# A recommendation tower on one core: ScalarE's and VectorE's orders redone around the pair copies, the first and the last pick, and the last relus

## The chip, the cores and the metric

The kernel runs on one core of a Trainium2 chip. The number that counts is the device time of one execution in microseconds (us). TensorE (PE), VectorE (DVE), ScalarE (ACT), GpSimd (POOL) and SyncE (SP) each work through their own list of instructions in order; they meet only at semaphores. PE's weight loads are shown as an engine of their own, PEld.

## The reference, cut to what matters

For each of 512 samples, 26 rows of 128 numbers are looked up by id (one per table) and joined by the dense vector to 27 vectors; the 351 products of two different ones are the features of a three-layer network.

```python
e = stack([tbl_f[ids[:, f]] for f in range(26)], axis=1)            # 512 x 26 x 128
all_vecs = concatenate([r_dense_proj[:, None, :], e], axis=1)        # 512 x 27 x 128
interactions = einsum('bnd,bmd->bnm', all_vecs, all_vecs)            # upper triangle: 351
h = concatenate([r_dense_proj, interact_flat, r_dense_proj], axis=1) # 512 x 607
h = maximum(h @ W_top1 + b_top1, 0)                                  # 512 x 512
h = maximum(h @ W_top2 + b_top2, 0)                                  # 512 x 256
y = h @ W_top3                                                       # 512 x 1
```

## The kernel before, in words

**Two ways to look up.** Fifteen tables are gathered by 60 indirect DMAs of POOL (4 tiles of 128 samples, 15 tables; line 227). They arrive with samples on partitions and are turned by PE (`turn`, line 270), then copied into `vecs` by ACT or, for two groups of the last tile, by DVE (`place_turned`, lines 454 and 587). The other eleven tables of 1000 rows are *picked*: a table lies in SBUF as 125 partitions x 8 rows, DVE compares the id's offset with 0 to 7 (`compare`, line 633) and PE multiplies the table with those one-hot columns (`pick`, line 255). A table goes through as a high part, which ACT casts (`split_table`, line 468), and a low part, which DVE subtracts (`make_low`, line 623); so a pick is 8 + 8 matmuls of 512 columns. The offsets come from `spread` (PE, line 242: ids laid over 125 partitions) and `find_offset` (ACT, line 460, which also needs `minus_first`, a small DMA). Until its first real work PE multiplies zeros (`keep_warm`, line 236).

**The last pick** (`LAST`, table 10 of the eleven) is done in two halves of 256 columns, with products of tile 0 between them, since tiles 0 and 1 need only the first half. Its one-hot columns are made 512 wide, as for every other pick.

**Then four tiles of 128 samples**, t = 0 to 3: `products` (line 293, 512 small matmuls of 27 x 27 in all) fills the bank pair `gram[t % 2]`; ACT (blocks of samples j = 0, 2) and DVE (j = 1, 3) copy the wanted rows into `pairs` in three layers of copies (`pairs_first` 8, `pairs_second` 8, `pairs_third` 4 copies per engine; line 445); `layer1` (lines 314 and 319) makes four slices of 128 hidden units in turn in two banks `shared[0]`, `shared[1]`, each emptied by an ACT relu (`relu1`, line 512); `layer2` (lines 334 and 342) and DVE's `relu2` (line 575); `layer3` (line 359) and `place_y` (line 581). In tiles 0 and 3 ACT takes one of DVE's copies over (`act_helps`).

**What sets the order.** The order of every engine is written out by hand, at the end of its block. A wait in the list holds up everything behind it on that engine. Layer 1's slice s needs the relu of slice s - 2 (same bank) and, in tiles 1 and 2, `relu2` of the tile before; its first slice waits for both engines' pair copies.

## Time and profile before

| | |
|---|---|
| runs of the kernel | 112.75, 113.46, 117.8 us (median 113.46) |
| profiled execution, its own time | 112.97 us |
| its span in the trace | 111.2 us |
| granted TensorE clock, mean | 0.998 of full speed |
| PE busy | 98.9 us (89%) |
| DVE busy | 75.0 us (67%) |
| ACT busy | 66.0 us (59%) |
| POOL busy | 62.4 us (56%) |

The busy shares are averages over unlike stages: up to about 53 us the picks, from there to 94 us the tiles, then a last stretch with nothing left to overlap. A row of the timeline gives start and duration in us, engine, line and operation, and in brackets the idle time before it and what ended it.

### The profile page before, as it was taken

What the parts mean: (1) busy time and instruction counts of PE and PEld (TensorE: products, weight loads), DVE (VectorE), ACT (ScalarE), POOL (GpSimd) and SP (SyncE); (2) the same over time, 40 slices, a digit from 0 to 9 for tenths busy, and PEclk for the clock granted to TensorE, in tenths of its full rate; (3) what the DMA queues carried; (4) which work ended last, traced back from release to release, by engine and by line L of the source; (5) the groups of instructions that cost most, each with busy time, mean ns of one, the idle gap of its engine ahead of it and who ended that gap; (6) DMA issues with size and microseconds to landing.
All of it is one profiled execution on the core that took longest, in us unless ns stands there. A gap on an engine that the chain in (4) does not pass through costs nothing.

```text
span 111.2 us, 3639 instructions
## 1 busy us (share of the span) xinstructions
PE 98.9 (89%) x1532; PEld 79.5 (72%) x1532; DVE 75.0 (67%) x205; ACT 66.0 (59%) x149; POOL 62.4 (56%) x68
## 2 busy tenths in 40 slices
PE   5999999999999999999789559889979997954982
PEld 2346667888887888888678459878978997924970
DVE  5269999899999999999006931992797200993021
ACT  3178999396468468446306994993797311595310
POOL 3877777777877777777777677767750000000000
PEclk9999999999999999999999999999999999999999
DMA  2899885476667679962222123222220000000000
GB/s 46 207 290 229 237 221 150 146 178 134 206 156 142 214 203 327 370 230 53 55 68 56 49 53 72 52 53 56 56 68 0 0 6 6 0 0 6 0 0 1
DMA packets 4936, 12.22 MB, mean 110 GB/s; under 512 B 2061, under 2 KB 2061, under 8 KB 4792
## 3 DMA queue, kind: packets, MB, share of 16 engines
q1 hardware_dynamic: 2848, 8.03, 24.7%
q0 software_dynamic: 1920, 3.94, 14.8%
q8 instruction: 12, 0.20, 0.8%
q10 hardware_dynamic: 152, 0.02, 0.2%
q14 instruction: 4, 0.03, 0.1%
HBM read 11.98 MB, written 0.00 MB: 108 GB/s over the span
## 4 chain that ended last, share of the span: by engine, by line
PE 69%; ACT 21%; DMA 4%; issue 3%; DVE 1%; ACTq 1%
PE shared L255 38%; ACT pairs L445 15%; PE gram L293 9%; PE shared L319 8%; DMA minus_first<-in_minus_first 4%; PE shared L334 4%; PE turned L270 3%; PE shared L314 2%; ACT h L512 2%; ACT vecs L454 2%; PE gram L342 1%; PE gram L242 1%; ACT vecs L477 1%; PE turned L359 1%; ACT table_hi L468 1%
## 5 line engine op out<-in xcount | busy, mean ns | idle before, releaser
L227 POOL DMA_INDIRECT rows<-in_tbl,ids x60 | 61.4, 1024 | 19.0 <-issue 18.0
L633 DVE TENSOR_SCALAR onehot<-offset 125x512 fp32r<-125x512 f16 x88 | 33.1, 435 | 3.7 <-ACT offset L460 2.9
L445 DVE COPY pairs<-gram 27x128 f32<-27x128 f32 (+6 forms) x78 | 22.6, 290 | 18.3 <-PE gram L293 17.1
L255 PE MATMUL shared<-onehot,table_hi 125*128 125x512 f32 (+1 forms) x96 | 26.2, 391 | 0.1
L445 ACT COPY pairs<-gram 27x128 f32<-27x128 f32 (+6 forms) x82 | 20.9, 255 | 9.1 <-PE gram L293 8.1
L255 PE MATMUL shared<-onehot,table_lo 125*128 125x512 f32 (+1 forms) x96 | 24.6, 378 | 0.0
L255 PEld LDWEIGHTS shared<-onehot,table_hi 125*128 125x128 f32 x96 | 16.8, 188 | 4.8 <-ACT table_hi L468 0.6
L255 PEld LDWEIGHTS shared<-onehot,table_lo 125*128 125x128 f32 x96 | 17.0, 188 | 4.2 <-DVE table_lo L623 0.7
L319 PE MATMUL shared<-pairs,w 128*128 128x128 f32 x128 | 17.0, 276 | 2.7 <-ACT pairs L445 2.7
L468 ACT CAST table_hi<-table 125x1024 fp32r<-125x1024 f32 x11 | 11.6, 1056 | 11.2 <-PE shared L255 10.4
L319 PEld LDWEIGHTS shared<-pairs,w 128*128 128x128 f32 x128 | 15.6, 192 | 2.9 <-ACT pairs L445 2.9
L293 PE MATMUL gram<-vecs 128*27 128x27 f32 x1024 | 12.3, 193 | 3.8 <-issue 2.3
L293 PEld LDWEIGHTS gram<-vecs 128*27 128x27 f32 x1024 | 10.5, 104 | 6.1 <-issue 4.3
L623 DVE TENSOR_TENSOR table_lo<-table,table_hi 125x512 fp32r<-125x512 f32 x22 | 14.8, 677 | 0.0
L472 ACT COPY vecs<-shared 128x512 f32<-128x512 f32 x10 | 12.2, 1218 | 1.5 <-PE shared L255 1.5
L512 ACT ACTIVATE h<-shared,b 128x128 f32<-128x128 f32 x16 | 5.7, 368 | 11.4 <-PE shared L319 11.4
L454 ACT COPY vecs<-turned 128x512 f32<-128x512 f32 (+1 forms) x14 | 9.4, 681 | 1.6 <-PE turned L270 1.5
L270 PE MATMUL turned<-identity,rows 128*128 128x128 f32 x60 | 9.4, 276 | 0.0
L314 PE MATMUL shared<-dense,w_dense 128*128 128x128 f32 x32 | 6.6, 287 | 1.8 <-ACT vecs L477 1.2
L270 PEld LDWEIGHTS turned<-identity,rows 128*128 128x128 f32 x60 | 7.1, 141 | 1.3 <-issue 0.4
L460 ACT ACTIVATE offset<-gram,minus_first 125x512 f16<-125x512 f32 x9 | 5.8, 685 | 2.6 <-DMA minus_first<-in_minus_first 2.6
L314 PEld LDWEIGHTS shared<-dense,w_dense 128*128 128x128 f32 x32 | 4.9, 191 | 2.2 <-issue 1.2
(36 smaller groups left out, 43.6 us busy)
## 6 DMA issues: line engine op xcount, KB each, us to landing
table<-in_tbl SPq DMA_DIRECT2D x11, 448.0 KB
w<-in_w_pairs SPq DMA_DIRECT2D x1, 1024.0 KB
rows<-in_tbl,ids POOLq DMA_INDIRECT x60, 3.6
table<-in_tbl SPq DMA_DIRECT2D x11, 52.0 KB
w_dense_both<-in_w_dense SPq DMA_DIRECT2D x1, 512.0 KB, 5.3
w<-in_w SPq DMA_DIRECT2D x1, 512.0 KB, 7.5
dense<-in_dense_t SPq DMA_DIRECT2D x1, 256.0 KB, 6.5
ids<-in_ids SPq DMA_DIRECT2D x1, 30.0 KB, 1.9
```

The source lines that it names most:

```text
L227: pool.indirect_dma_start(rows[:, t, f, :], None, a[f"tbl_{GATHER_TABLES[f]}"], bass.IndirectOffsetOnAxis(ids[:, t, f:f + 1], 0)).then_inc ...
L255: last = nc.tensor.matmul(out, (table_hi, table_lo)[part][u % 2][:, c, :], onehot[half][:, c - half * PIECE, cols], start=half == 0 and pa ...
L270: last = nc.tensor.transpose(turned[k % 2][:, u * 128:(u + 1) * 128], rows[:, t, f0 + u, :], identity[:, :])
L293: last = nc.tensor.matmul(gram[t % 2][32 * j:32 * j + VECS, o0:o0 + VECS], x, x, start=True, stop=True)
L314: nc.tensor.matmul(out, w1_dense[:, o], dense[:, cols], start=True, stop=False)
L319: last = nc.tensor.matmul(out, w1[:, c, o], pairs[:, c, cols], start=False, stop=c == CHUNKS - 1)
L445: last = copy(to[:, :, :, j, :], src[:, first:first + CHUNKS, :, :])
L454: nc.scalar.copy(vecs[:, t * TILE:(t + 1) * TILE, 1 + f0:1 + f0 + n], turned[k % 2][:, 0:n * 128].rearrange("d (n b) -> d b n", n=n)).then ...
L468: nc.scalar.copy(table_hi[u % 2][:, :, :], table[u % TABLE_BUFS][:, :, :]).then_inc(table_hi_ready, 1)
L472: nc.scalar.copy(vecs[:, :, 1 + GATHERED + u], shared[u % 2][:, :]).then_inc(picked_placed, 1)
L623: nc.vector.tensor_tensor(table_lo[u % 2][:, part, :], table[u % TABLE_BUFS][:, part, :], table_hi[u % 2][:, part, :].bitcast(fp32), ALU.s ...
L633: nc.vector.tensor_scalar(onehot[half][:, k, :], offset[:, u, :], float(half * PIECE + k), None, ALU.is_equal).then_inc(onehot_ready, 1)
```

## The change

ScalarE's list is rearranged: the pair copies of tiles 1 to 3 are cut into groups of four to eight, and relus of layer 1 and turned rows stand between the groups. `act_helps` goes: both engines make 20 pair copies in every tile. PE places `turn(3, 2)` ahead of `layer2(1)`, and `turn(3, 1)` between two halves of `layer1(1)`; slice 0 of `layer1(0)` no longer waits for the second half of the last pick. At the start, six warm-up matmuls, `spread(0)`, then five more, then the other spreads. The last pick's compares are 256 columns wide, the first 256 of all eight first. At the end the last tile's second relu goes to ACT, and layer 3's second part is cut in two (`Y_TILES`), one copied by ACT, one by DVE.

**ScalarE, tiles 1 and 2** (`h1_0`, `h1_1`: outputs of layer 1's relu for even and odd tiles; `gram1` holds the products of tile 1, `gram0` those of tile 2). Before, from tile 2's first copies on:

```order
L445 COPY pairs<-gram0 27x4x2x16 x8
L454 COPY vecs<-turned0 128x128x4
L512 ACTIVATE h1_1<-shared0,b1 128x128
L512 ACTIVATE h1_1<-shared1,b1 128x128
L445 COPY pairs<-gram0 19x4x2x16 x2
L445 COPY pairs<-gram0 22x4x2x16 x2
L445 COPY pairs<-gram0 10x4x2x16 x2
L445 COPY pairs<-gram0 14x4x2x16 x2
L512 ACTIVATE h1_1<-shared0,b1 128x128
L512 ACTIVATE h1_1<-shared1,b1 128x128
```

Now:

```order
L454 COPY pairs<-gram0 27x4x2x16 x4
L463 COPY vecs<-turned0 128x128x4
L516 ACTIVATE h1_1<-shared0,b1 128x128
L454 COPY pairs<-gram0 27x4x2x16 x4
L516 ACTIVATE h1_1<-shared1,b1 128x128
L454 COPY pairs<-gram0 19x4x2x16 x2
L454 COPY pairs<-gram0 22x4x2x16 x2
L516 ACTIVATE h1_1<-shared0,b1 128x128
L454 COPY pairs<-gram0 10x4x2x16 x2
L454 COPY pairs<-gram0 14x4x2x16 x2
L516 ACTIVATE h1_1<-shared1,b1 128x128
L463 COPY vecs<-turned0 128x128x4
```

The first relu of tile 1 stands behind four copies instead of eight, and each later one behind four more; the turned rows (3, 2) have come ahead of the tile's last four copies.

**TensorE, tile 1's second layer** (`turned0`, `turned1`: the two banks of turned rows, here groups (3, 1), (3, 2) and (3, 3)). Before, from slice 3 of `layer1(1)`:

```order
L314 MATMUL shared1<-dense,w1_dense 128x128
L319 MATMUL shared1<-pairs,w1 128x128 x4
L270 MATMUL turned1<-identity,rows 128x128 x4
L334 MATMUL shared0<-h1_1,w2 128x128 x4
L334 MATMUL shared1<-h1_1,w2 128x128 x4
L270 MATMUL turned0<-identity,rows 128x128 x4
L314 MATMUL shared0<-dense,w1_dense 128x128
```

Now:

```order
L318 MATMUL shared1<-dense,w1_dense 128x128
L323 MATMUL shared1<-pairs,w1 128x128 x4
L273 MATMUL turned0<-identity,rows 128x128 x4
L338 MATMUL shared0<-h1_1,w2 128x128 x4
L338 MATMUL shared1<-h1_1,w2 128x128 x4
L318 MATMUL shared0<-dense,w1_dense 128x128
```

Turn (3, 2), which stood behind the second layer of tile 1, now stands ahead of it; turn (3, 1) has gone up between slices 1 and 2.

**VectorE, the last pick** (`onehot0`, `onehot1`: one-hot columns for rows 0 to 3 and 4 to 7 of a partition). Of the change:

```order
L632 TENSOR_TENSOR table_lo0<-table1,table_hi0 125x512
L641 TENSOR_SCALAR onehot0<-offset 125x256 x4
L632 TENSOR_TENSOR table_lo0<-table1,table_hi0 125x512
L641 TENSOR_SCALAR onehot1<-offset 125x256 x4
L641 TENSOR_SCALAR onehot0<-offset 125x256 x4
```

Four more of `onehot1` follow. Before there were two groups of four, each 125x512, in the places of the first two.

The diff, cut to what the prediction speaks of:

```diff
-Y_TILES = [(0, 2), (2, 4)]
+Y_TILES = [(0, 2), (2, 3), (3, 4)]
-WARM_UPS = 9
+WARM_UPS = (6, 5)
-        y_sum = turned[0][0:1, :]
+        y_sum = [turned[0][0:1, :], turned[0][0:1, :], turned[1][0:1, :]]
@@ layer1
-                    pe.wait_ge(picked_placed, PICKED + 1)
                 for s in slices:
-                    if s < 2 and 1 <= t <= 2:
+                    if s < 2 and t == 0:
+                        pe.wait_ge(picked_placed, PICKED + s)
+                    elif s < 2 and t <= 2:
                         pe.wait_ge(h2_ready, S2 * (t - 1) + s + 1)
@@ TensorE's order
-            keep_warm(WARM_UPS, shared[0])
+            keep_warm(WARM_UPS[0], shared[0])
             pe.wait_ge(chooser_ready, 1)
             pe.wait_ge(pick_ids_half_ready, 1)
-            for u in range(SPREAD_BANKS):
+            spread(0)
+            keep_warm(WARM_UPS[1], shared[0])
+            for u in range(1, SPREAD_BANKS):
                 spread(u)
-            keep_warm(3, shared[1])
+            keep_warm(2, shared[1])
...
-            layer1(1)
+            layer1(1, [0, 1])
             turn(3, 1)
+            layer1(1, [2, 3])
+            turn(3, 2)
             layer2(1)
-            turn(3, 2)
...
             layer3(1)
+            layer3(2)
@@ ScalarE's order
             relu1(0, [0, 1])
-            pairs_first(1)
             place_turned(2, 2)
-            relu1(0, [2])
+            pairs_first(1, [0, 1])
             place_turned(2, 3)
-            relu1(0, [3])
+            relu1(0, [2, 3])
+            pairs_first(1, [2, 3])
             pairs_second(1)
             pairs_third(1)
-            pairs_first(2)
+            pairs_first(2, [0, 1])
             place_turned(3, 0)
-            relu1(1, [0, 1])
-            pairs_second(2)
-            relu1(1, [2, 3])
+            relu1(1, [0])
+            pairs_first(2, [2, 3])
+            relu1(1, [1])
+            pairs_second(2, [2, 3])
+            relu1(1, [2])
+            pairs_second(2, [0, 1])
+            relu1(1, [3])
+            place_turned(3, 2)
             pairs_third(2)
-            place_turned(3, 2)
-            relu1(2, [0, 1])
-            relu1(2, [2])
+            relu1(2, [0, 1, 2])
+            pairs_first(3)
             relu1(2, [3])
-            pairs_first(3)
             pairs_second(3)
             pairs_third(3)
             relu1(3)
+            act.wait_ge(h2_sum_ready, S2 * TILES)
+            nc.scalar.activation(h2[:, 1, 3 * TILE:4 * TILE], h2_sum(3, 1), ACT.Relu,
+                                 bias=b2[:, 1:2]).then_inc(h2_act_ready, 1)
+            act.wait_ge(y_sum_ready, 2)
+            nc.scalar.copy(y[:, Y_TILES[1][0] * TILE:Y_TILES[1][1] * TILE],
+                           y_sum[1][:, Y_TILES[1][0] * TILE:Y_TILES[1][1] * TILE]).then_inc(y_ready, 1)
@@ VectorE's order, the last pick
+            dve.wait_ge(offset_ready, PICKED)
+            make_low(LAST, 0)
+            compare(LAST, 0, slice(0, BATCH // 2))
+            make_low(LAST, 1)
+            compare(LAST, 1, slice(0, BATCH // 2))
+            compare(LAST, 0, slice(BATCH // 2, BATCH))
+            compare(LAST, 1, slice(BATCH // 2, BATCH))
...
-            relu2(3)
-            place_y(1)
+            relu2(3, [0])
+            place_y(2)
```

## Rows read from the trace of the kernel before

**Rows 1.** The chain that ended last, shares of the span by engine and line.

```profile
PE shared L255 38%; ACT pairs L445 15%; PE gram L293 9%; PE shared L319 8%; DMA minus_first<-in_minus_first 4%; PE shared L334 4%; PE turned L270 3%; PE shared L314 2%; ACT h L512 2%; ACT vecs L454 2%; PE gram L342 1%; PE gram L242 1%; ACT vecs L477 1%; PE turned L359 1%; ACT table_hi L468 1%
```

**Rows 2.** Timeline, the start: start, duration (us), engine, instruction, idle before.

```profile
1.20 3.94 PE L236 MATMUL shared<-blank 128*128 128x512 bf16 x9 [1.20 <-DVE blank L636]
...
3.23 0.35 DVE L640 CAST pick_ids_half<-pick_ids 11x512 f16<-11x512 int32 x1
...
5.80 0.69 ACT L460 ACTIVATE offset<-gram,minus_first 125x512 f16<-125x512 f32 x1 [2.62 <-DMA minus_first<-in_minus_first]
```

**Rows 3.** Timeline, the last pick.

```profile
48.62 1.47 DVE L633 TENSOR_SCALAR onehot<-offset 125x512 fp32r<-125x512 f16 x4
...
50.61 1.54 DVE L633 TENSOR_SCALAR onehot<-offset 125x512 fp32r<-125x512 f16 x4
...
51.21 1.39 PE L255 MATMUL shared<-onehot,table_hi 125*128 125x256 f32 x4
...
52.91 0.49 PE L270 MATMUL turned<-identity,rows 128*128 128x128 f32 x3
53.10 0.67 ACT L477 COPY vecs<-shared 128x256 f32<-128x256 f32 x1 [1.40 <-PE shared L255]
```

**Rows 4.** Groups by form: VectorE's copies of turned rows.

```profile
L587 DVE COPY vecs<-turned 128x512 f32<-128x512 f32 x1 | 0.7, 691 | 0.0
...
L587 DVE COPY vecs<-turned 128x384 f32<-128x384 f32 x1 | 0.6, 559 | 1.5 <-PE turned L270 1.5
```

**Rows 5.** Timeline, tile 0's pair copies and first layer.

```profile
59.17 3.04 DVE L445 COPY pairs<-gram 27x128 f32<-27x128 f32 x10 [6.42 <-PE gram L293]
...
64.80 0.66 ACT L477 COPY vecs<-shared 128x256 f32<-128x256 f32 x1
...
65.91 1.06 PE L319 MATMUL shared<-pairs,w 128*128 128x128 f32 x8
```

**Rows 6.** Timeline, up to tile 2's products.

```profile
70.84 1.06 PE L319 MATMUL shared<-pairs,w 128*128 128x128 f32 x8
...
72.59 1.82 PE L293 MATMUL gram<-vecs 128*27 128x27 f32 x128 [0.69 <-ACT vecs L454]
```

**Rows 7.** Timeline, tile 2's pair copies and tile 1's layers.

```profile
78.50 6.09 DVE L445 COPY pairs<-gram 27x128 f32<-27x128 f32 x20 [1.57 <-PE gram L293]
...
80.64 0.65 ACT L454 COPY vecs<-turned 128x512 f32<-128x512 f32 x1
...
81.17 0.63 ACT L512 ACTIVATE h<-shared,b 128x128 f32<-128x128 f32 x2
...
81.59 0.49 PE L314 MATMUL shared<-dense,w_dense 128*128 128x128 f32 x2 [0.63 <-ACT h L512]
...
84.65 2.05 PE L334 MATMUL shared<-h,w 128*128 128x128 f32 x16
...
86.98 0.39 PE L314 MATMUL shared<-dense,w_dense 128*128 128x128 f32 x2
```

**Rows 8.** Timeline and POOL's line over 60 to 90 us: the gathers.

```profile
77.60 0.94 POOL L227 DMA_INDIRECT rows<-in_tbl,ids  x1 [0.30 <-issue]
...
DMA to landing us min/median/max: 2.4/2.5/3.7
```

**Rows 9.** Timeline, tile 3's pair copies.

```profile
94.22 5.81 DVE L445 COPY pairs<-gram 27x128 f32<-27x128 f32 x19 [5.04 <-PE gram L293]
...
95.85 5.60 ACT L445 COPY pairs<-gram 27x128 f32<-27x128 f32 x21
...
101.50 1.16 PE L319 MATMUL shared<-pairs,w 128*128 128x128 f32 x8 [2.73 <-ACT pairs L445]
```

**Rows 10.** Timeline, the end.

```profile
107.61 0.61 DVE L575 TENSOR_SCALAR h<-gram,b 128x128 f32<-128x128 f32 x2 [6.62 <-PE gram L342]
108.11 1.02 PE L359 MATMUL turned<-h,w 128*1 128x256 f32 x4 [0.31 <-DVE h L575]
109.17 0.41 DVE L581 COPY y<-turned 1x256 f32<-1x256 f32 x1 [0.95 <-PE turned L359]
```

More of the change, by code:

```diff
@@ L155, in build_dlrm @@
         gram_ready = sem("gram_ready")
-        quarter_free = sem("quarter_free")
+        h2_act_ready = sem("h2_act_ready")
         layer_act = sem("layer_act")
@@ L243, in spread, with pick @@
                                  ).then_inc(spread_ready, 1)
-            def pick(u, half, cols=slice(0, BATCH), bank_no=None):
+            def pick(u, half, cols=slice(0, BATCH), bank_no=None, earlier=None):
+                made = PER_PART * (u if earlier is None else earlier)
                 out = shared[u % 2 if bank_no is None else bank_no][:, cols]
@@ L251, in pick @@
                         if part == 0:
-                            pe.wait_ge(onehot_ready, PER_PART * u + c + 1)
+                            pe.wait_ge(onehot_ready, made + c + 1)
                         elif c % LOW_PART == 0:
@@ L352, in layer3 @@
                     pe.wait_ge(turned_act, turns_before(NG * TILES, False))
+                elif k == 1:
+                    pe.wait_ge(y_ready, 1)
                 else:
-                    pe.wait_ge(y_ready, k)
+                    pe.wait_ge(turned_dve, turns_before(NG * TILES, True))
                 cols = slice(t0 * TILE, t1 * TILE)
                 for o in range(S2):
-                    pe.wait_ge(h2_ready, S2 * (t1 - 1) + o + 1)
-                    last = nc.tensor.matmul(y_sum[:, cols], w3[:, o:o + 1], h2[:, o, cols],
+                    if k == 2 and o == 1:
+                        pe.wait_ge(h2_act_ready, 1)
+                    else:
+                        pe.wait_ge(h2_ready, S2 * (t1 - 1) + o + 1)
+                    last = nc.tensor.matmul(y_sum[k][:, cols], w3[:, o:o + 1], h2[:, o, cols],
                                             start=o == 0, stop=o == S2 - 1)
@@ L397, in _ @@
             pe.wait_ge(picked_placed, PICKED - 1)
-            pick(LAST, 0, second, (LAST + 1) % 2)
+            pick(LAST, 0, second, (LAST + 1) % 2, PICKED)
             products(0, 1)
-            pick(LAST, 1, second, (LAST + 1) % 2).then_inc(picked_ready, 1)
+            pick(LAST, 1, second, (LAST + 1) % 2, PICKED).then_inc(picked_ready, 1)
             turn(2, 0)
@@ L431, in _ @@
             layer3(1)
-        def act_helps(t):
-            return t in (0, TILES - 1)
+            layer3(2)
         def put_pairs(copy, t, js, layer, q):
@@ L498, in pairs_third @@
                 put_pairs(nc.scalar.copy, t, (0, 2), 2, 2)
-                last = put_pairs(nc.scalar.copy, t, (0, 2), 2, 3)
-                if act_helps(t):
-                    act.wait_ge(quarter_free, t // (TILES - 1) + 1)
-                    last = put_pairs(nc.scalar.copy, t, (1,), 2, 2)
-                last.then_inc(pairs_act, 1)
+                put_pairs(nc.scalar.copy, t, (0, 2), 2, 3).then_inc(pairs_act, 1)
             def relu1(t, slices=range(S1)):
-                if t >= 2:
+                if t >= 2 and slices[0] == 0:
                     act.wait_ge(h2_sum_ready, S2 * (t - 1))
@@ L568, in _, with relu2 @@
             relu1(3)
+            act.wait_ge(h2_sum_ready, S2 * TILES)
[4 more added lines that the diff above has]
+                           y_sum[1][:, Y_TILES[1][0] * TILE:Y_TILES[1][1] * TILE]).then_inc(y_ready, 1)
         @block.vector
         def _(dve):
-            def relu2(t):
-                for o in range(S2):
+            def relu2(t, sums=range(S2)):
+                for o in sums:
                     dve.wait_ge(h2_sum_ready, S2 * t + o + 1)
@@ L580, in place_y @@
                 cols = slice(Y_TILES[k][0] * TILE, Y_TILES[k][1] * TILE)
-                nc.vector.tensor_copy(y[:, cols], y_sum[:, cols]).then_inc(y_ready, 1)
+                nc.vector.tensor_copy(y[:, cols], y_sum[k][:, cols]).then_inc(y_ready, 1)
             def place_turned(t, g):
@@ L607, in pairs_third @@
                 dve.wait_ge(layer_dve, 2 * t + 2)
-                if act_helps(t):
-                    put_pairs(nc.vector.tensor_copy, t, (1,), 2, 3).then_inc(quarter_free, 1)
-                    put_pairs(nc.vector.tensor_copy, t, (3,), 2, 2)
-                    put_pairs(nc.vector.tensor_copy, t, (3,), 2, 3).then_inc(pairs_dve, 1)
-                else:
-                    put_pairs(nc.vector.tensor_copy, t, (1, 3), 2, 2)
-                    put_pairs(nc.vector.tensor_copy, t, (1, 3), 2, 3).then_inc(pairs_dve, 1)
+                put_pairs(nc.vector.tensor_copy, t, (1, 3), 2, 2)
+                put_pairs(nc.vector.tensor_copy, t, (1, 3), 2, 3).then_inc(pairs_dve, 1)
             def make_low(u, i):
@@ L625, in make_low, with compare @@
                                         ).then_inc(table_lo_ready, 1)
-            def compare(u, half):
+            def compare(u, half, cols=slice(0, BATCH)):
                 if u >= 1:
@@ L632, in compare @@
                 for k in range(PIECE):
-                    nc.vector.tensor_scalar(onehot[half][:, k, :], offset[:, u, :], float(half * PIECE + k),
+                    nc.vector.tensor_scalar(onehot[half][:, k, cols], offset[:, u, cols], float(half * PIECE + k),
                                             None, ALU.is_equal).then_inc(onehot_ready, 1)
@@ L645, in _ @@
             make_low(0, 1)
-            for u in range(1, PICKED):
+            for u in range(1, PICKED - 1):
                 make_low(u, 0)
```

## The prediction, made before the changed kernel ran

> **What bounds the kernel now.** I read the chain of waits first, then the timeline around each edit. The chain [rows 1] is PE's picks for 38% of the span; behind them PE's layers take turns with ACT's pair copies (15%) on one path. So the picks give nothing unless a wait sits in them, and in the tiles the question is each time which of three lists, PE's, ACT's or DVE's, is late. The timeline gives, by place: the first offset ends a wait for `minus_first` [rows 2]; the last pick's third group of matmuls is stretched [rows 3]; `layer1(0)`, `products(2, 0)` and `layer1(1)` wait for work on ACT [rows 5 to 7]; in tile 3 ACT ends the copies 7.28 us after DVE began them [rows 9].
>
> **Base.** The profiled execution took 112.97 us, 1.8 more than its span; the median of the runs shown is 113.46. The sum goes against 112.97. About 2% (2.3 us) is what a measurement of this kernel can tell from no change.
>
> **The start: 0.** Nine warm-ups come 0.43 us apart from 1.20 on, so `spread(0)` starts at 5.07. Behind six it starts at 3.8, the ids being ready at 3.58. But the offset at 5.80 ended its wait with `minus_first`'s landing [rows 2], which nothing here moves. Ids alone would be worth at most the three warm-ups, 1.3; so 0 to 1.3, and I take 0, by the row's own releaser. The other spreads come later; PE has slack until the first table is cast.
>
> **The last pick: 0.9.** Its last four compares start at 50.61 and come (1.54 - 0.44) / 3 = 0.36 apart, so the third group of four matmuls, 51.21 [rows 3], takes 1.39 instead of about 0.64 (4 x 0.117 and the last one's tail): PE stands 0.75 to 0.9 behind its data. No row shows a compare of 256 columns. Bounds: the full pitch of 0.35, then nothing is gained (0), and the size's share. DVE's copies of 512 and 384 columns differ by 132 ns [rows 4], so 0.16 of 0.69 is fixed; a compare's 0.44 then has 0.27 that goes with the columns, and half of it off leaves a pitch of 0.21 to 0.22. The first four end at 49.6, `make_low` at 50.1, the next four by 51.1, as PE gets there. PE runs through, the turn at 52.91 comes at 52.0: 0.9. Second halves, eight more compares, are done by 52.8 and the dense weights by 53.5; PE wants the former at 54.7. The Trainium skill ("VectorE: DVE Perf Modes", the TRN2 errata) speaks against this edit: every operation out of SBUF pays a fixed latency again, so small ones should be avoided; it gives 150 cycles as the fixed term measured. By that a half compare takes about 0.29 us (an estimate from that page), and with nothing of it overlapped this term would be 0.8, not 0.9.
>
> **Tile 0: 0.6.** Pair copies start 0.9 earlier, 58.3. DVE's 20 copies take 6.09 (as in [rows 7]) and set the end, 64.38; ACT's 20 at 0.267 ((5.60 - 0.26) / 20, [rows 9]) end at 63.6. Before, `layer1(0)` waited for all of the last pick, placed by ACT at 64.80 to 65.46 behind 21 copies, and began its pair matmuls at 65.91 [rows 5]. Now slice 0 needs the pairs alone and its dense matmul runs ahead: 64.41. 1.5 earlier in all, 0.6 of it new. Slice 1 needs ACT's placing, done by 64.3.
>
> **Up to `products(2, 0)`: 0.8.** Before, PE's slice 3 was issued by 71.73 (70.84 and 8 x 0.111), then PE waited to 72.59 for turned rows (2, 3) [rows 6], behind eight copies, a turned copy and a relu. Shifted by 1.5 PE is there at 70.23. ACT now: turn (2, 2) out at 67.85, placed by 68.4 (0.53, the step from 80.64 to 81.17 in [rows 7]), four copies to 69.5, rows (2, 3) by 70.1. No wait: 70.25, 2.3 earlier. The deferred relus end at 70.8; `layer2(0)` wants them at 72.2. ACT's other 16 copies end at 75.1, before tile 2's products.
>
> **Tile 1's layers: 0.6.** Tile 2's copies start at 78.50 - 2.34 = 76.16. PE: slices 0 and 1 no longer wait for eight copies; slice 1 out at 78.5, turn 78.9, slices 2 and 3 by 81.2, turn (3, 2) by 81.6. ACT from 76.16: four copies (1.07), turned rows (0.53), relu (0.26), then three times four copies and a relu (1.33 each; the last relu in full, 0.37): 82.1. So `layer2(1)` starts at 82.15, not 84.65, and the turn of 0.44 that stood behind it is gone: `layer1(2)` begins at 84.04, not 86.98 [rows 7]. 2.94 earlier, 0.6 of it new. Here ACT is late by 0.5; behind that relu wait only the turned rows and four copies, done at 83.6, wanted at 84.3. DVE ends its copies at 82.25 and its turned rows at 82.9, in time for `relu2(1)`.
>
> **Tile 3's copies: 1.15.** To `products(3, 1)` nothing else changes: DVE starts at 91.28. Both engines start together now; DVE's 20 take 6.09 and end at 97.37, ACT's, with slice 3's relu among them, at 96.9. The pair matmuls start at 97.41 instead of 101.50 [rows 9]: 4.1.
>
> **The end: 0.5.** Before, second sum to span end: relu twice, four passes of 256 columns (0.22 each and a tail), a copy of 256: 1.97 from 107.61 [rows 10]. Now layer 3's tile 2 fills PE while both relus run side by side; its own 128 columns cost 0.45 and a tail of 0.17, the copy about 0.28. Some 1.47: 0.5, with 0.2 to 0.6 as ends.
>
> **Sum:** 0 + 0.9 + 0.6 + 0.8 + 0.6 + 1.15 + 0.5 = 4.6 (rounded). 112.97 - 4.6 = **108.4 us**, span 106.6. ACT, DVE and PE each lose slack; what is late next is DVE, whose 20 copies at 0.305 end every tile's copies.
>
> **Rivals.**
> 1. *ACT's mixed list becomes the bound* (chance 0.13). Each relu in it waits for PE and holds copies behind it. For it: the relu that releases `layer2(1)` is 0.5 late even in my sum. Against: ACT's 20 copies are 0.75 shorter than DVE's. If relus, once mixed, miss their slots, the terms of 0.8 and 0.6 are lost, and with some of the last pick's: 110.0 to 110.7.
> 2. *The start pays too* (0.12): in executions where `minus_first` lands sooner, the ids are what is late, and up to 1.3 comes off. For: both are within 0.8 us of one another. Against: the releaser named. Gathers cap it: turn (3, 2)'s rows are issued up to 77.60 and land 2.5 later, 80.1 [rows 8], and it runs at 81.2 in my sum: 107.3.
> 3. *Gathers stop PE ahead of `layer2(1)`*, the side of slower (0.03; another 0.06 for a loss that ends within 2%). POOL's rate is fixed by its own 60 instructions, and turn (3, 2), which had 6 us of slack, now has 1.1 and stands in front of the second layer; ACT's placing of it stands in front of the last four copies of tile 2. Past 1.1 each us of lateness costs one: with the slowest landing shown, 3.7 [rows 8], 0.1. To be slower than before the rows must land 4.6 + 1.1 us late, 8.2 us after issue; at 113.5 and more that is slower, from 115.3 it would be measurable. The profile has no such landing. 
>
> The main case has the rest, 0.62; alone it holds 107.6 to 109.3.
>
> **Numbers.** The time is the main case's, 108.4. Range 107.2 to 110.3: below by the gathers' cap, above by the loss of the last pick or of one tile's term and half of another's; it leaves out the worse half of rival 1 and rival 3. Faster by over 2% (under 110.7 against the profiled execution) is the main case, rivals 2 and 4, and most of 1: 0.88. Within 2%: 0.09. Slower: 0.03.
>
> **What would show it.** The first offset still released by `minus_first`, near 5.8. The third group of the last pick under 0.8 us. `products(2, 0)` without an ACT releaser. `layer2(1)` 2.5 earlier, released by an ACT relu and not by a DMA. Tile 3's pair matmuls about 6.1 us behind DVE's first copy, with DVE as releaser. Relus of the last tile on two engines, 1.5 us to the last copy. It is wrong if turn (3, 2) waits for a gather, if ACT's copies end later than DVE's in any tile, or if compares of 256 columns come 0.35 apart.

## The result, and the profile after

| | before | changed |
|---|---|---|
| executions measured in turn | 112.75, 113.46, 117.8, 118.49 us | 109.6, 109.61, 109.75, 110.15 us |
| ratio, with its 95% interval | | 0.9706 [0.9635, 0.9776] |
| profiled execution, its own time | 112.97 us | 110.15 us |
| its span | 111.2 us | 108.3 us |
| PE busy | 98.9 us (89%) | 99.3 us (92%) |

The median, 109.68, is faster by some 3%, inside the range and 1.3 us above the forecast. Between the profiled executions 2.8 us are gone, where the sum had 4.6. An execution more than 1.5% above the fastest of its kernel is left out of every ratio here, which is why a ratio and a quotient of medians differ.

The chain of waits of the changed kernel, shares of the span by engine and line:

```profile
PE shared L258 38%; PE shared L323 12%; DVE pairs L454 11%; PE gram L296 10%; PE turned L273 5%; PE shared L238 5%; PE shared L338 4%; PE gram L244 3%; PE shared L318 3%; PE gram L346 2%; PE turned L368 1%; ACT pairs L454 1%; ACT h L516 1%; ACT vecs L486 1%; PE turned L244 0%
```

Against [rows 1], ACT's pair copies fell from 15% to 1%, and DVE's stand in their place with 11%. `minus_first` has left the chain, although it still ends the first offset's wait.

Timeline, the start and the last pick (answers to [rows 2, 3]):

```profile
3.87 0.68 PE L244 MATMUL gram<-pick_ids_half,chooser 11*125 11x512 f16 x1
...
5.63 0.69 ACT L469 ACTIVATE offset<-gram,minus_first 125x512 f16<-125x512 f32 x1 [2.45 <-DMA minus_first<-in_minus_first]
...
48.63 1.01 DVE L641 TENSOR_SCALAR onehot<-offset 125x256 fp32r<-125x256 f16 x4
...
50.16 2.74 DVE L641 TENSOR_SCALAR onehot<-offset 125x256 fp32r<-125x256 f16 x12
...
51.28 0.63 PE L258 MATMUL shared<-onehot,table_hi 125*128 125x256 f32 x4
...
52.22 0.49 PE L273 MATMUL turned<-identity,rows 128*128 128x128 f32 x3
```

`spread(0)` starts 1.2 earlier, and the offset still goes where `minus_first` lets it, at 5.63. The stretched group of 1.39 has become 0.63. Twelve compares of 256 columns take 2.74, a pitch of 0.22.

Timeline, tile 0 to tile 2's products ([rows 5, 6]):

```profile
58.58 6.09 DVE L454 COPY pairs<-gram 27x128 f32<-27x128 f32 x20 [5.09 <-PE gram L296]
...
64.82 1.13 PE L323 MATMUL shared<-pairs,w 128*128 128x128 f32 x8 [1.05 <-DVE pairs L454]
...
70.81 1.26 PE L296 MATMUL gram<-vecs 128*27 128x27 f32 x96
```

`products(2, 0)` has no releaser any more: PE runs into it.

Timeline, tile 2's copies and tile 1's layers ([rows 7]); this stretch decides the case:

```profile
76.78 6.09 DVE L454 COPY pairs<-gram 27x128 f32<-27x128 f32 x20 [1.78 <-PE gram L296]
...
78.40 0.36 ACT L516 ACTIVATE h<-shared,b 128x128 f32<-128x128 f32 x1
78.78 1.05 ACT L454 COPY pairs<-gram 27x128 f32<-27x128 f32 x4
78.93 1.16 PE L323 MATMUL shared<-pairs,w 128*128 128x128 f32 x8 [0.58 <-issue]
...
80.13 0.37 ACT L516 ACTIVATE h<-shared,b 128x128 f32<-128x128 f32 x1 [0.29 <-PE shared L323]
...
83.00 0.37 ACT L516 ACTIVATE h<-shared,b 128x128 f32<-128x128 f32 x1
...
83.42 2.05 PE L338 MATMUL shared<-h,w 128*128 128x128 f32 x16 [0.23 <-ACT h L516]
...
85.31 0.39 PE L318 MATMUL shared<-dense,w_dense 128*128 128x128 f32 x2
```

`layer2(1)` is released by ACT's fourth relu, as forecast, but starts 6.64 us behind DVE's first pair copy; it was 6.15 before [rows 7], and the working had 5.99. At 78.93 PE stands idle for 0.58 and waits for nothing that the profile can name ("issue").

Timeline, tile 3 and the end ([rows 9, 10]):

```profile
92.00 0.94 PE L296 MATMUL gram<-vecs 128*27 128x27 f32 x88 [0.98 <-issue]
...
92.99 6.09 DVE L454 COPY pairs<-gram 27x128 f32<-27x128 f32 x20 [5.47 <-PE gram L296]
...
99.22 1.13 PE L323 MATMUL shared<-pairs,w 128*128 128x128 f32 x8 [1.45 <-DVE pairs L454]
...
105.31 0.35 DVE L589 TENSOR_SCALAR h<-gram,b 128x128 f32<-128x128 f32 x1 [5.27 <-PE gram L346]
...
105.53 0.37 ACT L578 ACTIVATE h<-gram,b 128x128 f32<-128x128 f32 x1 [1.42 <-PE gram L346]
...
106.49 0.28 DVE L595 COPY y<-turned 1x128 f32<-1x128 f32 x1 [0.83 <-PE turned L368]
```

In tile 3 the wait is DVE's and 1.45 instead of 2.73. But ahead of it PE stands for 0.98 in `products(3, 1)`.

**The time by stretches** is the view that answers the forecast. Each stretch runs from DVE's first pair copy of a tile to that of the next; the last one ends with the last copy. The repeats are the changed kernel again (told of below), on two chips. In us:

| stretch | before | changed | repeat 1 | repeat 2 | gain forecast | gain measured |
|---|---|---|---|---|---|---|
| start to tile 0's copies | 59.17 | 58.58 | 58.61 | 59.16 | 0.9 | 0.6, 0.6, 0.0 |
| tile 0 to tile 1 | 9.89 | 9.45 | 9.46 | 9.47 | 0.6 | 0.4 in each |
| tile 1 to tile 2 | 9.44 | 8.75 | 8.70 | 8.68 | 0.8 | 0.7, 0.7, 0.8 |
| tile 2 to tile 3 | 15.72 | 16.21 | 15.52 | 15.74 | 0.6 | -0.5, 0.2, 0.0 |
| tile 3 to the last copy's end | 15.36 | 13.78 | 13.79 | 13.78 | 1.65 | 1.6 in each |

Tile 0's row came 0.16 short, the third and the last within 0.1. The first came in part or not at all. The fourth did not come against this trace of the kernel before, but one trace is a poor measure of it: the other two traces with the old order of tile 1 (`start_only` and `old_tiles`, below) have 16.16 and 16.05, so 15.98 is the mean of the three. Eight with the new order (the three here, `cmp_whole`, `old_t3`, `old_end`, `old_start` and `help0`) lie between 15.45 and 16.21, with a mean of 15.70. By the means the fourth gain is 0.3, half of the forecast.

### The profile page after: what moved, and what is told of

Same layout as the page of the kernel before. It is cut to its first block, busy times and chain, and to the rows that moved or that the text cites. A ratio compares the mean times of both kernels' runs of the same rounds, so it can differ in the third digit from the quotient of the medians.

```text
span 108.3 us, 3655 instructions
## 1 busy us (share of the span) xinstructions
PE 99.3 (92%) x1536; PEld 80.5 (74%) x1537; DVE 76.0 (70%) x214; ACT 66.5 (61%) x149; POOL 62.5 (58%) x68
## 4 chain that ended last, share of the span: by engine, by line
PE 81%; DVE 11%; issue 3%; ACT 2%; DVEq 0%
PE shared L258 38%; PE shared L323 12%; DVE pairs L454 11%; PE gram L296 10%; PE turned L273 5%; PE shared L238 5%; PE shared L338 4%; PE gram L244 3%; PE shared L318 3%; PE gram L346 2%; PE turned L368 1%; ACT pairs L454 1%; ACT h L516 1%; ACT vecs L486 1%; PE turned L244 0%
## 5 line engine op out<-in xcount | busy, mean ns | idle before, releaser
L641 DVE TENSOR_SCALAR onehot<-offset 125x512 fp32r<-125x512 f16 (+1 forms) x96 | 34.0, 415 | 3.5 <-ACT offset L469 2.8
L454 DVE COPY pairs<-gram 27x128 f32<-27x128 f32 (+6 forms) x80 | 23.2, 290 | 16.9 <-PE gram L296 15.7
L454 ACT COPY pairs<-gram 27x128 f32<-27x128 f32 (+6 forms) x80 | 20.4, 255 | 9.3 <-PE gram L296 8.3
L258 PE MATMUL shared<-onehot,table_hi 125*128 125x512 f32 (+1 forms) x96 | 25.5, 387 | 0.0
L296 PE MATMUL gram<-vecs 128*27 128x27 f32 x1024 | 13.2, 193 | 2.4 <-issue 1.2
L296 PEld LDWEIGHTS gram<-vecs 128*27 128x27 f32 x1024 | 11.0, 104 | 5.0 <-issue 3.7
L238 PE MATMUL shared<-blank 128*128 128x512 bf16 x13 | 5.3, 559 | 1.2 <-DVE blank L644 1.2
```

The costliest lines, as they stand in the source:

```text
L238: nc.tensor.matmul(free_bank[:, 0:512], blank[:, 0:128], blank[:, :], start=True, stop=True)
L258: last = nc.tensor.matmul(out, (table_hi, table_lo)[part][u % 2][:, c, :], onehot[half][:, c - half * PIECE, cols], start=half == 0 and pa ...
L296: last = nc.tensor.matmul(gram[t % 2][32 * j:32 * j + VECS, o0:o0 + VECS], x, x, start=True, stop=True)
L454: last = copy(to[:, :, :, j, :], src[:, first:first + CHUNKS, :, :])
L641: nc.vector.tensor_scalar(onehot[half][:, k, cols], offset[:, u, cols], float(half * PIECE + k), None, ALU.is_equal).then_inc(onehot_ready, 1)
```

## The experiments

The questions were two: do the parts bring in their own stretches what the sum says, and what are the idle times on PE that nothing ends? My theory for the second, formed from the traces: **PE's own instructions are supplied in blocks**, and a block takes over 3 us to come. PE works through 128 products in 1.3 to 2.2 us, and then stands until the next block is there. Four windows of the changed kernel from the span's start (PE alone: window, length, busy time and count of matmuls, clock, DMA share, GB/s); the last three end where an idle time without a releaser ends, the first 126 matmuls ahead of the second:

```profile
0.00:54.70 54.70, 52.88 (x343) 1.00 0.70 192
...
0.00:57.84 57.84, 55.74 (x469) 1.00 0.67 185
...
0.00:78.92 78.92, 74.62 (x1101) 1.00 0.55 151
...
0.00:91.99 91.99, 86.48 (x1354) 1.00 0.48 132
```

469 and 1101 are 632 apart, 1101 and 1354 are 253: five and two times 126 to 127. A matmul and its weight load are two instructions. From 343 to 469 it is 3.1 us, of which PE works 2.9 (55.74 - 52.88). In the same way the idle time of 1.26 in the kernel before ends 4.1 us behind the one ahead of it, 127 matmuls back (58.6 to 62.7). The profile's page has a DMA queue of the kind "instruction"; it moved 12 packets, and the program has 1536 matmuls with 1537 weight loads, 256 of these instructions to a packet. In the windows 55.0 to 55.5, 76.5 to 77.0 and 89.5 to 90.0 the queue's row (packets, MB, share of the 16 DMA engines' time) is:

```profile
q8 instruction: 1, 0.02, 12.5%
q8 instruction: 1, 0.02, 11.9%
q8 instruction: 1, 0.02, 10.9%
```

So one packet starts in each (narrower windows put them at 55.35, 76.60 and 89.78) and takes 0.9 to 1.0 us (11.9% of 16 times 0.5 us is 0.95). PE goes on 1.3 to 1.5 us after its end, at 57.84, 78.92 and 91.99. The rival: those idle times belong to the gathers or to other traffic, and not to the count.

**Repeats.** `a0` and `a1` are the changed kernel without an edit (an empty line in `a1`). `a0` shares its chip with `s15`, `s63` and `old_tiles`, `a1` with `help0`, `start_only` and `pe_stream`; the chip of `cmp_whole`, `old_t3`, `old_end` and `old_start` has no repeat of the changed kernel, so their whole times can be set only against the kernel before.

> The changed kernel again, as the measure for the others of this run. Its trace showed TensorE idle for 0.58 us with no releaser in layer1(1) (78.93) and for 0.98 us in products(3, 1) (92.00). Supply theory (TensorE's own instructions come in blocks of 256, each asked for when the one before it is entered and there 3.1 to 4.2 us later): the gaps stand again behind matmul 469, 1101 and 1354 or next to them, each within 0.5 us of its size. Rival, chance (a disturbance of that one execution): they are elsewhere or gone, and the span is 107.2 or less.

Measured: 108.83 to 109.72 in five executions, a sixth 113.22; ratio 0.9621 [0.9564, 0.9679]. The idle times stand behind matmul 469, 1101 and 1354 again, with a fourth behind 596; chance is excluded.

> The changed kernel again, as the measure for the others of this run: 109.2 to 109.8 us, 4 us below the kernel before.

Measured: 109.27 to 110.21 in five, a sixth 113.52; ratio 0.9703 [0.9636, 0.977]; the median is 0.3 above what was expected. So the change is worth 3 to 4%, 3.3 to 4.3 us, and two chips (medians 109.4 and 110.09) differ by half of what the working was off. PE's idle times without a releaser in `a0` (but for one of 0.16), two of the three in `a1`, and two of the three in the kernel before:

```profile
57.97 0.37 PE L296 MATMUL gram<-vecs 128*27 128x27 f32 x25 [0.31 <-issue]
...
61.52 0.51 PE L296 MATMUL gram<-vecs 128*27 128x27 f32 x38 [0.18 <-issue]
...
78.50 1.16 PE L323 MATMUL shared<-pairs,w 128*128 128x128 f32 x8 [0.15 <-issue]
...
91.30 0.94 PE L296 MATMUL gram<-vecs 128*27 128x27 f32 x88 [0.65 <-issue]
```

```profile
58.53 0.37 PE L296 MATMUL gram<-vecs 128*27 128x27 f32 x25 [1.32 <-issue]
...
92.06 0.94 PE L296 MATMUL gram<-vecs 128*27 128x27 f32 x88 [0.86 <-issue]
```

```profile
62.69 0.51 PE L293 MATMUL gram<-vecs 128*27 128x27 f32 x37 [1.26 <-issue]
...
93.25 0.93 PE L293 MATMUL gram<-vecs 128*27 128x27 f32 x87 [0.56 <-issue]
```

The same matmuls each time (25, 38 and 88 left of a group of products; 37 and 87 in the kernel before, whose start has one matmul less), with other lengths. The 1.32 is why repeat 2 gained nothing in the first stretch.

**Instructions added at the start.** `s15`: the five warm-ups behind `spread(0)` become twenty of 128 columns, 15 pairs more and the same columns. `s63`: five become forty of 64 columns, and six become twenty-four of 128, 53 pairs more. The edit of `s15`:

```diff
-            keep_warm(WARM_UPS[1], shared[0])
+            keep_warm(WARM_UPS[1], shared[0], 128)
```

> Changed: the five warm-up matmuls behind the first spread are twenty of a quarter of the width, so TensorE has 15 matmuls and 15 weight loads more, in the same time, before everything else. Supply theory: every block boundary falls 15 matmuls earlier in the program. The one at 1101 is then reached about 1.5 us sooner after the one before it (15 matmuls of layer 1 at 0.11 us), so its gap grows from 0.6 to 1 or 2 us and lies at the end of products(2, 1) or in turn(3, 0); the one in products(3, 1) stays near 1 us. Time +0.3 to +1.2 us. Rival (the gaps come from what the instructions do, or from gathers and table loads beside them): gaps stay at the same instructions, time within 0.2 us of the changed kernel's.

Measured: median 111.39; ratio 0.9771 [0.9717, 0.9825]. By the executions that the ratios use it is 1.8 us longer than `a0`, more than the 0.3 to 1.2 expected. The profiled execution, 115.92 us, is one of the long ones: up to some 13 us its matmuls took nearly twice as long (the first four of the first pick 2.27 against 1.28), and tile 0's copies start at 62.26 instead of 58.6, which shifts every later time. Its idle times:

```profile
65.15 0.86 PE L296 MATMUL gram<-vecs 128*27 128x27 f32 x53 [0.70 <-issue]
...
81.81 0.49 PE L273 MATMUL turned<-identity,rows 128*128 128x128 f32 x3 [1.49 <-issue]
...
82.52 1.92 PE L323 MATMUL shared<-pairs,w 128*128 128x128 f32 x8
...
97.56 1.06 PE L296 MATMUL gram<-vecs 128*27 128x27 f32 x103 [0.64 <-issue]
```

38 left has become 53, 88 has become 103: each idle time moved by exactly the 15 pairs that were added 60 to 90 us earlier, and from the span's start each stands behind the same count as ever, 596, 1101 and 1354. That is what a theory of counts says and no theory of places or traffic does. The one at 81.81 fell into `turn(3, 0)`, where it cost its 1.49 and the halved clock behind it (0.50 granted from 82.5 to 84.4; eight pair matmuls in 1.92 instead of 1.06).

> Changed: five warm-ups become forty of an eighth of the width, the six before them twenty-four of a quarter: 53 more matmuls and weight loads before everything else, in the same time. Supply theory: all boundaries fall 53 matmuls earlier: the gap in layer1(1) is gone from there (the boundary is inside products(2, 1)), and products(3, 0) holds a boundary near its end with a gap of 0.3 to 1 us; in all between -0.6 and +0.6 us. Rival (gaps belong to the instructions or to the DMAs beside them): same places, same time within 0.2 us.

Measured: 110.21 to 117.15, median 112.32, and my number missed: all six executions lie above `a0`'s median of 109.4, by 0.8 us to 7.8 us, not by up to 0.6. Its first two idle times:

```profile
56.97 1.38 PE L296 MATMUL gram<-vecs 128*27 128x27 f32 x78 [0.37 <-issue]
61.07 1.19 PE L296 MATMUL gram<-vecs 128*27 128x27 f32 x91 [0.71 <-issue]
```

25 + 53 = 78 and 38 + 53 = 91. The count holds again. As expected, the idle time in `layer1(1)` is gone; the one expected near the end of `products(3, 0)` isn't there, but one of 0.82 stands 13 matmuls before the end of `products(3, 1)`, a block further on. Two more, of 1.43 and 0.90, fell into `products(1, 1)` and `products(2, 0)`. The five together are 4.2 us, against 1.8 in the changed kernel's profiled execution (0.23, 0.58 and 0.98). So where the boundaries fall matters, and this shift made it worse.

**The supply by itself.** `pe_stream` leaves the network out (its output is zero): PE issues 2400 products of 27 columns (two records each) on zeros with nothing to wait for, beside the 60 gathers and then, from some 80 us on, with no gather.

> Not the network: TensorE does nothing but 2400 matmuls of 27 x 27 (4800 in the trace, as each is made in two passes) on zeros, one after the other, while POOL makes its 60 gathers and then nothing; the output is zero. Supply theory: 4800 pairs of weight load and matmul are 38 blocks of 127 pairs; a block lasts 1.8 us at 14 ns a pair but needs 3.1 to 4.2 us to arrive, so TensorE goes at 127 pairs in 3.1 to 4.2 us, with an idle stretch without releaser in every block, 118 to 160 us in all. Rival (the gaps come from other engines' work beside it): it runs through at 14 ns a pair, 67 us, and the end is set by the gathers at 75 to 85 us.

Measured: 136.95 us, in the one execution made. Timeline at 75 to 80 us, then the group of all (line, count, busy time and mean ns, idle before), then the queue:

```profile
75.23 1.90 PE L104 MATMUL gram<-blank 128*27 128x27 f32 x128 [1.43 <-issue]
...
78.69 1.71 PE L104 MATMUL gram<-blank 128*27 128x27 f32 x128 [1.55 <-issue]
```

```profile
L104 PE MATMUL gram<-blank 128*27 128x27 f32 x4800 | 69.5, 226 | 64.0 <-issue 62.8 <-DVE blank L110 1.1
```

```profile
q8 instruction: 37, 0.61, 1.8%
```

4800 records of matmuls take 69.5 us and PE stands idle for 62.8 more, behind the first 223 and then behind each 128 of them, every 3.45 to 4.0 us, and no less where no gather runs. 37 packets of 16 KB (0.61 MB) fit 4800 pairs at about 128 to a packet, and the queue keeps step with PE: packets start at 72.90, 76.34 and 79.81, each 1.1 us behind the start of a group of 128 (71.78, 75.23, 78.69), take 0.9 to 1.1, and PE goes on 1.3 to 1.4 after their end. The rival, 67 us beside gathers alone, is excluded. That PE stands for want of its own instructions is shown. One thing differs from the network: the granted clock was 0.50 from 10 us on. In the network, at 1.00, a block took about as long, 3.1 to 4.2 us.

**Parts undone.** Each kernel is the changed one with one part as before.

`old_tiles`: ACT's order in tiles 1 and 2 and PE's around `layer2(1)`.

```diff
-            layer1(1, [0, 1])
+            layer1(1)
             turn(3, 1)
-            layer1(1, [2, 3])
+            layer2(1)
             turn(3, 2)
-            layer2(1)
...
-            pairs_first(2, [0, 1])
+            pairs_first(2)
             place_turned(3, 0)
-            relu1(1, [0])
-            pairs_first(2, [2, 3])
-            relu1(1, [1])
-            pairs_second(2, [2, 3])
-            relu1(1, [2])
-            pairs_second(2, [0, 1])
-            relu1(1, [3])
+            relu1(1, [0, 1])
+            pairs_second(2)
+            relu1(1, [2, 3])
+            pairs_third(2)
```

> The changed kernel with ScalarE's order of tiles 1 and 2, and TensorE's order of turn(3, 1), turn(3, 2) and layer 1 of tile 1, as in the kernel before; all else is kept. By the prediction's terms (0.8 and 0.6 of it are this) the time is 1.4 us longer. By what the changed kernel's trace shows (a gap of 0.6 us stands where TensorE no longer waits for relus), 0.7 to 0.9 us longer: the gap in layer1(1) is hidden in the relus' wait that comes back. Rival, ACT's mixed list costs as much as it gives: within 0.3 us.

Measured: ratio 0.974 [0.9672, 0.9808], median 111.1; by the executions that the ratios use, 1.4 us above `a0` on the same chip, as the terms say, though the stretches give only 0.7 and 0.3. Its profiled execution, 114.36 us, is one of the long ones (tile 0's copies at 62.31), so only the stretches behind that are read. Tile 1 to tile 2 takes 9.39 again instead of 8.7, 0.7 of the forecast's 0.8; tile 2 to tile 3 takes 16.05, against 15.45 to 16.21 with the new order. Its second layer of tile 1 starts 6.33 behind the first copy, 0.17 of which is a wait of ACT's second relu for PE:

```profile
81.15 6.09 DVE L453 COPY pairs<-gram 27x128 f32<-27x128 f32 x20 [1.40 <-PE gram L296]
...
87.48 2.05 PE L338 MATMUL shared<-h,w 128*128 128x128 f32 x16 [0.30 <-ACT h L515]
```

`cmp_whole`: the last pick's compares in 512 columns.

```diff
-            for u in range(1, PICKED - 1):
+            for u in range(1, PICKED):
                 make_low(u, 0)
...
-            compare(LAST, 0, slice(0, BATCH // 2))
```

> The changed kernel with the last pick's one-hot columns made 512 wide again, in the old order. By the prediction's term 0.9 us longer. By the changed kernel's trace (the turn behind the pick's first half at 52.22, before at 52.91) 0.7 longer. Rival: the pair copies of tile 0 start when TensorE's instructions for products(0, 1) are there, not when the pick ends, and most of it is hidden: 0.3 or less.

Measured: median 110.65; ratio 0.9659 [0.9568, 0.9751], which can't be told from those of `a0` and `a1`. In its trace:

```profile
51.52 1.34 PE L258 MATMUL shared<-onehot,table_hi 125*128 125x256 f32 x4
...
53.17 0.49 PE L273 MATMUL turned<-identity,rows 128*128 128x128 f32 x3
```

The stretched group is back. The turn stands at 53.17 instead of 52.22 to 52.30, but the pick itself began later too (50.49 against 50.25 to 50.33), which is no matter of the compares. From its first matmul to the turn it takes 2.68, and 1.96 to 1.98 in every trace with the new compares; the kernel before and `start_only` have 2.77. So the compares are worth 0.7 to 0.8, of the 0.9 forecast. What arrives at tile 0's copies depends on PE's idle times behind the pick (0.68 here, 0.23, 0.31 and 1.32 in the three traces of the changed kernel).

`old_t3`: `act_helps` back in tiles 0 and 3, and slice 3's relu ahead of tile 3's copies.

```diff
+            return t in (0, TILES - 1)
...
             relu1(2, [0, 1, 2])
+            relu1(2, [3])
             pairs_first(3)
-            relu1(2, [3])
```

> The changed kernel with ScalarE taking one of VectorE's pair copies over in tiles 0 and 3 again (21 and 19), and with tile 2's last relu ahead of tile 3's first copies. By the prediction's term for tile 3, 1.15 us longer. With tile 0 counted too, where VectorE's 20 copies now end last (64.67, ScalarE's 63.94): there the old shares would let the first pair matmuls start about 0.3 earlier, so 0.7 to 0.9 us longer in all. Rival (relus and copies on ScalarE cost as much either way): within 0.3 us.

Measured: median 111.39; ratio 0.9711 [0.9607, 0.9815]. Tile 3 to the end takes 14.82 instead of 13.78: 1.0 of the forecast 1.15. The releaser is ACT again:

```profile
92.22 5.81 DVE L459 COPY pairs<-gram 27x128 f32<-27x128 f32 x19 [5.46 <-PE gram L297]
93.79 5.62 ACT L459 COPY pairs<-gram 27x128 f32<-27x128 f32 x21
...
99.46 1.16 PE L324 MATMUL shared<-pairs,w 128*128 128x128 f32 x8 [2.69 <-ACT pairs L459]
```

`old_end`: one engine for the last relus, layer 3 in two parts.

```diff
-Y_TILES = [(0, 2), (2, 3), (3, 4)]
+Y_TILES = [(0, 2), (2, 4)]
...
-            relu2(3, [0])
-            place_y(2)
+            relu2(3)
+            place_y(1)
```

> The changed kernel with the old ending: both relus of the last tile and both copies of y on VectorE, layer 3 in two parts of 256 columns. By the prediction and by the changed kernel's trace (1.46 us from the second sum to the last copy's end, before 1.97) 0.5 us longer. Rival, ScalarE's late relu and copy cost what the cut saves: 0.2 or less.

Measured: median 111.15; ratio 0.9694 [0.9599, 0.9788]. In its profiled execution (113.7 us, tile 0's copies at 62.23, so again only the stretches behind count) tile 3 to the end takes 14.28: 0.5 more, the forecast term to a tenth.

`old_start`: warm-ups (9, 0) and 3. `start_only`: the kernel before with the new start alone.

```diff
-WARM_UPS = (6, 5)
+WARM_UPS = (9, 0)
...
-            keep_warm(2, shared[1])
+            keep_warm(3, shared[1])
```

> The changed kernel with nine warm-ups ahead of the first spread, none behind it and three at the end, as before. By the prediction, no difference. By the changed kernel's trace, TensorE reaches the first pick 0.34 us earlier (7.48 against 7.82), which VectorE's compares swallow to 0.1 by the last pick: 0 to 0.2 us shorter. Rival (the ids pay in executions where minus_first lands sooner): up to 1.3 us longer.

> The kernel before with only the new start (six warm-ups, the first spread, five warm-ups, the other spreads, two warm-ups). By the prediction no difference (0), since the first offset waits for minus_first. By the clock theory: in the start of before TensorE stands still ahead of the first pick, and the granted clock averaged 0.97 to 0.985 in most of its executions, which costs 1.5 to 4 us each; with no pause left the clock is 1.0 in nearly all, so the median of all executions falls by 1.5 to 2.5 us while the quickest stay at 113.3 to 113.8. Rival (the clock falls by chance, whatever the start): as many executions under 0.99 as the kernel before has.

Measured: `old_start` 111.02, ratio 0.9675 [0.9533, 0.9818], not to be told from the changed kernel's. `start_only` against the kernel before, 13 executions: 1.0047 [0.9986, 1.0107]. The start is worth nothing, as forecast: at most 0.2 us in the executions of that ratio. Its trace has tile 0's copies at 59.19, before had 59.17. The clock theory of that expectation is refuted: 8 of the 13 executions had a mean granted clock under 0.99, and 10 of 17 of the kernel before on that chip.

**A version that may be better.** `help0` gives ACT back its 21st copy in tile 0 alone, where its list has no relu between the copies.

```diff
+        def act_helps(t):
+
+            return t == 0
```

> The changed kernel with ScalarE taking over one of VectorE's copies in tile 0 alone (21 and 19), not in tile 3. There VectorE's 20 copies end at 64.7 and hold TensorE; 19 end 0.3 earlier, ScalarE's 21 at 64.2. If VectorE's end is what holds tile 0, 0.3 us shorter. Rival, TensorE's instruction supply takes it back in the tiles behind: no difference (0.1 or less).

Measured: 108.58, 109.0, 109.19, 110.15, 110.21, 110.39; ratio 0.97 [0.9623, 0.9776]. Its profiled execution is the shortest of all:

```profile
58.21 5.80 DVE L459 COPY pairs<-gram 27x128 f32<-27x128 f32 x19 [5.07 <-PE gram L297]
...
64.16 1.13 PE L324 MATMUL shared<-pairs,w 128*128 128x128 f32 x8 [0.44 <-DVE pairs L459]
```

The first pair matmul starts 5.95 behind DVE's first copy, against 6.24 in the changed kernel: 0.3, as expected. `old_t3`, which has the same split in tile 0, gives 5.96. The whole stretch from tile 0 to tile 1 is 8.95 here and 9.49 in `old_t3`, against 9.45 to 9.47, so what follows the first pair matmul scatters by as much as the gain. In the whole time nothing can be told (median 109.67 against `a1`'s 110.09).

## Why the prediction was right and where it failed

**The step that failed is "Tile 1's layers: 0.6".** The stretch from DVE's first copy of tile 2 to that of tile 3 falls into three parts (us; the first three columns have the old order of tile 1, the last three the new one):

| part | before | `start_only` | `old_tiles` | changed | repeat 1 | repeat 2 |
|---|---|---|---|---|---|---|
| first copy to `layer2(1)` | 6.15 | 6.17 | 6.33 | 6.64 | 6.28 | 6.30 |
| `layer2(1)` to `layer1(2)` | 2.33 | 2.33 | 2.33 | 1.89 | 1.89 | 1.89 |
| `layer1(2)` to tile 3's first copy | 7.24 | 7.66 | 7.39 | 7.68 | 7.35 | 7.55 |
| of it, idle in `products(3, 1)` | 0.56 | 0.97 | 0.70 | 0.98 | 0.65 | 0.86 |

*The first part was to lose 0.16* (5.99 instead of 6.15) and grew by 0.13 to 0.15 where nothing disturbed it, and by 0.49 in the profiled execution. `layer2(1)` waits for the fourth relu, and ahead of that relu ACT has the same work in both orders: 16 pair copies, one block of turned rows, three other relus. Moving relus between copies can't bring the last one forward. I added up pitches of rows from steady stretches, and each was a little short: a copy behind a relu comes 0.38 or 0.39 later in two of three places (78.40 to 78.78), where I had 0.26. That is a mis-sized term, and rival 1's mechanism at a small price. In the profiled execution the idle time of 0.58 in `layer1(1)` held ACT's second relu back by 0.29 more.

*The second part was to lose 0.44*, by the turn that left the path, and did, in every trace.

*Of the third part the prediction says "To `products(3, 1)` nothing else changes".* By the means nothing did (7.43 in the three traces with the old order, 7.46 in the eight with the new). But 7.24, which I carried over from the trace of before as fixed work, holds an idle time of PE without a releaser, and it was the shortest of all thirteen traces of the network; `start_only`, with the same order there, has 7.66. So the part is 0.44 longer in the profiled execution by chance and not by the change, and that hid the second part's gain. With chance set aside the term of 0.6 is worth 0.44 less 0.14, that is 0.3. Of the 1.7 us by which the two profiled spans fall short of the sum, 1.1 lie in this term: 0.3 mis-sized, 0.8 from idle times of PE that vary from one execution to the next.

The other points:

- **Start, 0**: right, by `start_only`. In every trace with the new start `minus_first` ends the first offset's wait, between 5.29 and 6.05 (before it was 5.80). Rival 2's 1.3 us would need a wait that ends near 4.5; none did.
- **Last pick, 0.9**: a little large, 0.7 to 0.8 by itself (`cmp_whole`). The pitch was right: four compares take 1.01 and twelve 2.74, so 0.216 each, where 0.21 to 0.22 was worked out from VectorE's copies, and 0.36 for the last of a row. Between the start and tile 0's copies 0.6, 0.6 and 0.0 arrived: the first pick stood 0.34 later in the profiled execution, of which 0.11 was left at the last pick, and `a1` stood for 1.32 at 58.53. The Trainium skill ("VectorE: DVE Perf Modes", the TRN2 errata) gave 0.29 a compare by its fixed term as an estimate; here the measurement decides, 0.216 in a row.
- **Tile 0, 0.6**: 0.44. DVE sets it, as said; PE's first pair matmul starts 0.15 behind DVE's last copy (58.58 + 6.09 = 64.67 to 64.82), where I had 0.03.
- **Up to `products(2, 0)`, 0.8**: 0.7 to 0.8, without a releaser, and undone with its part.
- **Tile 3, 1.15 and the end, 0.5**: 1.6 together, in all three traces of the changed kernel; undone singly 1.0 and 0.5.
- **Gathers**: no turn waits for one, so rival 3 is excluded.
- **"DVE ends every tile's copies"** holds in tiles 0 and 3 only. In the profiled execution ACT ends later in tile 1 (75.60 against 74.12) and in tile 2 (85.00 against 82.87), as the prediction's own working had it (75.1; 83.6 against 82.25). No wait hangs on these ends, so its sign "wrong if ACT's copies end later in any tile" was badly chosen.

The term that failed was a difference of a few tenths between two long sums. The terms that held were single waits with a releaser in the trace. Luck went against the forecast here: the profiled execution drew a long third part, and the kernel before the shortest.

**What stays open.** Why a block of instructions takes 3.1 us in one place and 4.2 in another, and so how large these idle times are in a given execution. Over all of PE they came to 2.3 us before and 1.9, 1.5 and 2.3 with the change, so the sum of them did not grow; what changed is which lie on the path (the 1.26 of before, up to 62.69, lies ahead of a wait of 1.16 for ACT that ended at 65.61, and so cost next to nothing).

## What to carry to other kernels

Book a saved wait only as far as the next floor, and look for floors in the trace's idle times that have no releaser: they are not work, and they don't shift with it. Before crediting a reorder on an engine, count what stands ahead of the instruction that is waited for; if that is the same in both orders, it will come at the same time at best. And take the base of a term of tenths from more than one trace. Divide the time by stretches between fixed events, over several executions: undoing a part then shows in its own stretch to a tenth or two, where the whole time can't tell it.

## What the runs showed of the hardware

- **TensorE's instructions come in blocks** of about 127 pairs of weight load and matmul, 3.1 to 4.2 us a block in the network and 3.45 to 4.0 in `pe_stream`. A stream of small matmuls (128 in 1.6 to 2.1 us) outruns it and leaves PE half idle; the picks' matmuls of 512 columns don't, and have no such idle time.
- **An idle time can cost more than itself.** In `start_only`'s profiled execution PE waited 2.75 us for tile 3's pair copies and went on at the lower of its two levels, 1.2 GHz. Windows (length, busy time and count of PE, its weight loads, DVE, ACT and POOL, then granted clock, DMA share, GB/s):

```profile
100.00:103.00 3.00, 1.01 (x5) 1.02 (x5) 1.41 (x5) 1.85 (x8) 0.00 (x0) 0.72 0.03 5
103.00:105.00 2.00, 2.00 (x11) 2.00 (x11) 0.00 (x0) 0.37 (x1) 0.00 (x0) 0.50 0.00 0
```

  The granted clock was 0.50 from 103 to 108, where the kernel before had 1.00, and tile 3 to the end took 18.30 instead of 15.36. Over all executions, with that wait at 2.7 us (the kernel before, `start_only`, `old_t3`) 35 of 55 had a mean clock under 0.99; with it at 1.45 and the new start (the changed kernel, `a0`, `a1`, `old_tiles`, `cmp_whole`, `old_end`, `help0`) none of 40 had. `s15` (3 of 7), `s63` (1 of 6) and `old_start` (2 of 5) show it with the short wait too: behind the 1.49 in a turn in `s15`, and in `old_start` behind a wait of 0.88 ahead of the first pick (0.50 granted from 8 to 10). So the median of all executions gains more than the ratio says, some 6 us (115.63 to 109.68). That the fall comes behind the wait of 2.7 is seen in the one trace of `start_only`; for the other 34 executions it is argued from the counts.
